# Attention phases of a two-layer kernel: the side work of a phase dealt out over other steps, and the group norm applied on another engine

## The reference, cut to what matters

```python
x = x + _L0_conv_ref(_gn(x), Wq, Wk, Wv, Wo, ln_g, ln_b)
# _gn: group norm, 32 groups of 8 channels over all positions of one image
q = xf @ Wq.T;  k = xf @ Wk.T * SCALING;  vr = xf @ Wv.T        # per head
qr = theta_shift(q, sin_q, cos_q);  kr = theta_shift(k, sin_k, cos_k)
qk = einsum('bhqd,bhkd->bhqk', qr, kr) * mask
den = clip(abs(qk).sum(-1, keepdims=True), 1.0, 50000.0)
out = einsum('bhqk,bhkd->bhqd', qk / den, vr)
out = (out - mu) / sqrt(var + LN_EPS) * ln_g + ln_b             # per head
out = gelu(out) @ Wo.T
```

## Time and profile before

| what | value |
|---|---|
| median of 3 runs | 2482.15 us (2479.42 to 2482.56) |
| the profiled execution | 2484.05 us, span 2482.3 us, granted clock 0.995 |
| PE busy | 2360.1 us, 95% |
| DVE busy | 1811.6 us, 73% |
| ACT busy | 1457.4 us, 59% |
| POOL busy | 1053.4 us, 42% |
| chain that ended last | PE 89%, DVE 7%, issue 2%, ACT 1% |

### The profile page before, as it was taken

How to read it: one execution, slowest core, us unless ns; L and a number is a source line. 1 busy time by engine, 2 the same in 40 slices (tenths; PEclk the granted TensorE clock), 3 DMA queues, 4 the chain that set the end, 5 groups by cost and what they waited for, 6 DMA issues and landing times.

```text
span 2482.3 us, 38646 instructions
## 1 busy us (share of the span) xinstructions
PE 2360.1 (95%) x14870; PEld 1617.3 (65%) x14870; DVE 1811.6 (73%) x2772; ACT 1457.4 (59%) x2063; POOL 1053.4 (42%) x758
## 2 busy tenths in 40 slices
...
GB/s 240 86 73 91 97 88 97 89 97 89 97 90 96 89 97 100 98 66 71 97 94 65 68 111 26 26 26 26 26 26 26 26 26 24 17 17 22 26 26 17
DMA packets 89271, 165.74 MB, mean 67 GB/s; under 512 B 21488, under 2 KB 62840, under 8 KB 80768
## 3 DMA queue, kind: packets, MB, share of 16 engines
...
...
## 4 chain that ended last, share of the span: by engine, by line
PE 89%; DVE 7%; issue 2%; ACT 1%; POOL 0%; another core or an unknown queue 0%; DVEq 0%; POOLq 0%; ACTq 0%
PE scores L1747 9%; PE scores L1745 9%; PE scores L1746 9%; PE scores L418 9%; PE pairC L431 8%; PE pairC L450 5%; PE pairD L347 5%; DVE l_prod L560 4%; PE pairD L356 2%; PE pairC L1745 2%; PE pairC L1746 2%; PE pairC L1747 2%; PE pairD L1745 2%; PE pairD L1747 2%; PE pairD L1746 2%
## 5 line engine op out<-in xcount | busy, mean ns | idle before, releaser
L560 DVE TENSOR_TENSOR l_prod<-scores,l_window 128x1024 f32<-128x1024 f32 x512 | 602.9, 1219 | 198.0 <-PE scores L418 194.4
L773 ACT ACTIVATE l_absp<-l_prod 128x1024 f32<-128x1024 f32 x512 | 539.6, 1055 | 296.1 <-DVE l_prod L560 285.2
L2135 POOL TENSOR_TENSOR e_xnorm<-e_res,e_scale 128x1024 f32<-128x1024 f32 x16 | 38.9, 2434 | 775.3 <-DMA e_res<-t2T_scratch 775.3
L1904 ACT ACTIVATE e_r<-scores,e_bn,e_rs 128x512 f32<-128x512 f32 x256 | 197.9, 779 | 273.2 <-PE scores L1747 273.1
L881 POOL TENSOR_TENSOR l_absp<-l_absp,l_absp 128x1024 f32<-128x1024 f32 x126 | 297.5, 2384 | 5.7 <-ACT l_absp L773 5.7
L2011 DVE CAST e_h1hi<-e_r 128x512 fp32r<-128x512 f32 x256 | 147.7, 577 | 206.4 <-ACT e_r L1904 206.2
L1914 ACT ACTIVATE e_r<-scores,e_bn,e_rs 128x512 f32<-128x512 f32 x250 | 194.7, 781 | 136.8 <-PE scores L1747 135.5
L431 PE MATMUL pairC<-l_prod,l_v 128*32 128x512 f32 x2048 | 270.3, 600 | 0.0
L418 PEld LDWEIGHTS scores<-l_qhi,l_khi 32*128 32x128 f32 x1024 | 49.5, 181 | 319.9 <-DVE l_prod L560 221.2
L2038 DVE TENSOR_TENSOR e_r<-e_r,e_wbc 128x512 f32<-128x512 f32 x250 | 170.8, 691 | 84.8 <-ACT e_r L1914 84.7
L418 PE MATMUL scores<-l_qhi,l_khi 32*128 32x512 f32 x1024 | 129.3, 494 | 96.5 <-DVE l_prod L560 95.8
(11 more groups left out here) (256 smaller groups left out, 5284.3 us busy)
## 6 DMA issues: line engine op xcount, KB each, us to landing
l_absp<-l_absp POOLq DMA_DIRECT2D x63, 1024.0 KB, 7.1
...
l_xa<-x_scratch SPq DMA_DIRECT2D x8, 1024.0 KB, 8.3
l_xr<-x_scratch SPq DMA_DIRECT2D x8, 1024.0 KB, 5.6
t2T_scratch<-l_xt SPq DMA_DIRECT2D x8, 1024.0 KB, 14.9
...
```

The costliest lines, as they stand in the source:

```text
L560: nc.vector.tensor_tensor(prod[2 * (S % 2) + j][:], sc[j][:], win[:, 4 * g + 2 * j:4 * g + 2 * j + 2, w0:w0 + QC], ALU.mult).then_inc(prod ...
L773: nc.scalar.activation(absp[S % ABS][j][:], prod[2 * (S % 2) + j][:], ACT.Abs).then_inc(abs_ready, 1)
L1904: nc.scalar.activation(r1[:, m, :], p1[m], ACT.Relu, bias=bn_[0][1][:, m, n:n + 1], scale=rs[0][:, m, n:n + 1]).then_inc(r1_ready, 1)
```

## The change

- **DMA and POOL pairs.** DMAs now add steps 0+1 and 2+3, POOL 4+5 and 6+7. PE takes the pairs in steps 6, 6, 7 and 9 (in places p=1, where `has_gn` holds, in 5, 7, 7 and 9). The last phase keeps its old split. `weighted` now comes ahead of `sums` in a step.
- **PE side tasks.** v is projected in step 5 (6 where `has_gn` holds). Of the output projections, places 0, 1, 2 and 3 had one, one, two and none; now each has one, in step 4, but for the last two phases.
- **DVE.** head_sums moves from step 2 to step 1, behind the shuffle; centre from 3 to 2; variance from 4 to 3; the residual stands at step 5 ahead of `group_mean`, not at step 6; the image's four `statistics` stand in other steps; `normalise` is gone. `group_mean` has one more small instruction, the negated mean.
- **ACT.** take_num is ahead of absolute(S, 0) in step 0, take_den ahead of it in step 2, squares in step 2, high of k in step 1 of the next phase. `normalise` is here, one activation for each half of the channels, with a shift that POOL makes (`l_gshift`).
- **POOL.** low of k moves behind the last pair of the phase; scale_heads stands between the DMA of 2+3 and the adds of 4+5; the rotation of k behind the adds.
- **Buffers.** t1 and t2 are doubled, one set for q and one for k; the squares have their own buffer; z has a spare piece.

The diff, without the memory map and renamed buffers:

```diff
     def by_dma(P):
-        return (0, 4) if P < PHASES - 1 else (0,)
+        return (0, 2) if P < PHASES - 1 else (0,)
 
     def by_pool(P):
-        return (2, 6) if P < PHASES - 1 else (2,)
+        return (4, 6) if P < PHASES - 1 else (2,)
+
+    def has_gn(P):
+        return P % 4 == 1 and P // 4 + 1 < B
 
     def den_at(P):
 
-        if P < PHASES - 1:
-            return {5: (0, 1), 6: (2, 3), 8: (4, 5), 9: (6, 7)}
-        return {4: (0, 1), 5: (2, 3), 6: (4,), 7: (5,), 8: (6,), 9: (7,)}
-
-    units = sorted((KT * P + at, tuple(KT * P + s for s in steps)) for P in range(PHASES) for at, steps in den_at(P).items())
-    units_at = {at: steps for at, steps in units}
+        if P == PHASES - 1:
+            return ((5, (0, 1)), (5, (2, 3)), (6, (4,)), (7, (5,)), (8, (6,)), (9, (7,)))
+        if has_gn(P):
+            return ((5, (0, 1)), (7, (2, 3)), (7, (4, 5)), (9, (6, 7)))
+        return ((6, (0, 1)), (6, (2, 3)), (7, (4, 5)), (9, (6, 7)))
+
+    units = sorted((KT * P + at, tuple(KT * P + s for s in steps)) for P in range(PHASES) for at, steps in den_at(P))
+    units_at = {S: [steps for at, steps in units if at == S] for S in range(KT * PHASES + 2)}
...
-        return {0: [(b, 0, 0)], 1: [(b, 0, 1)], 2: [(b, 1, 0), (b, 1, 1)], 3: []}[P % 4]
+        if P >= PHASES - 2:
+            return [(b, 1, 0), (b, 1, 1)] if P == PHASES - 2 else []
+        return [(b, P % 4 // 2, P % 2)]
...
             if kt == 5 and len(outs(P)) == 2:
                 out_proj(*outs(P)[1], (part,))
-            if kt == 6 and has_kv(P):
+            if kt == (6 if has_gn(P) else 5) and has_kv(P):
...
-            if S in units_at:
-                sums(units_at[S])
             weighted(S)
+            for steps in units_at[S]:
+                sums(steps)
...
+            nc.vector.tensor_scalar(gneg[:], pA[:, 0:2], -1.0, None, ALU.mult).then_inc(gneg_ready, 1)
...
+            if kt == 1 and has_q(P):
+                shuffle(prep_q(P))
+            if kt == 1 and P > 0:
+                head_sums(P - 1)
+            if kt == 2 and P > 0:
+                centre(P - 1)
             if kt == 3 and P > 0:
-                centre(P - 1)
-            if kt == 4 and P > 0:
+                clip_den(P - 1)
                 variance(P - 1)
-            if kt == 6 and outs(P):
-                add_residual(*outs(P)[-1])
-            if kt == 7 and p == 0 and stats_next:
-                statistics(b + 1, (1,))
+            if kt == 4 and has_kv(P):
+                shuffle(prep_k(P))
+            if kt == 5 and outs(P):
+                add_residual(*outs(P)[0])
+            if kt == 6 and len(outs(P)) == 2:
+                add_residual(*outs(P)[1])
+            if kt == 5 and has_gn(P):
+                group_mean(b + 1, a_order["gn1", P])
+            if kt == 6 and has_gn(P):
+                group_var(b + 1, a_order["gn2", P])
+            if kt in (5, 6, 7) and p == 0 and stats_next:
+                statistics(b + 1, (kt - 5,))
             if kt == 0 and p == 1 and stats_next:
                 statistics(b + 1, (3,))
-            if kt == 1 and has_q(P):
-                shuffle(prep_q(P))
-            if kt == 1 and p == 1 and stats_next:
+            if kt == 2 and p == 1 and stats_next:
                 aggregate(b + 1)
-            if kt == 1 and p == 2 and stats_next:
-                normalise(b + 1, (0,))
-            if kt == 2 and p == 2 and stats_next:
-                normalise(b + 1, (1,))
-            if kt == 2 and P > 0:
-                head_sums(P - 1)
-            if kt == 3 and P > 0:
-                clip_den(P - 1)
-            if kt == 4 and has_kv(P):
-                shuffle(prep_k(P))
-            if kt == 5 and p == 0 and stats_next:
-                statistics(b + 1, (0,))
-            if kt == 5 and has_gn(P):
-                group_mean(b + 1, a_order["gn1", P])
-            if kt == 5 and len(outs(P)) == 2:
-                add_residual(*outs(P)[0])
-            if kt == 6 and has_gn(P):
-                group_var(b + 1, a_order["gn2", P])
-            if kt == 7 and p == 0 and stats_next:
-                statistics(b + 1, (2,))
...
-            if n > 0:
-                act.wait_ge(lo_ready, n)
+            if n > 1:
+                act.wait_ge(lo_ready, n - 1)
             act.wait_ge(a_ready, a + 1)
-            nc.scalar.activation(t1[:], pA[:], ACT.Copy, scale=scale).then_inc(t1_ready, 1)
+            nc.scalar.activation(t1[n % 2][:], pA[:], ACT.Copy, scale=scale).then_inc(t1_ready, 1)
...
-            act.wait_ge(a_ready, a_order["dT", P] + 1)
             act.wait_ge(centred, P + 1)
-            nc.scalar.activation(tB[:], tA[:], ACT.Square, scale=HD ** -0.5).then_inc(sq_ready, 1)
+            nc.scalar.activation(sq[:], tA[:], ACT.Square, scale=HD ** -0.5).then_inc(sq_ready, 1)
+
+        def normalise(b, k):
+
+            act.wait_ge(grstd_ready, 2 * (b + 1))
+            nc.scalar.activation(xn[:, k, :], raw[:, k, :], ACT.Identity, bias=gshift[:, k:k + 1],
+                                 scale=grstd[:, k:k + 1]).then_inc(xn_ready, 1)
 
...
+            b, p = P // 4, P % 4
+            if kt == 0 and P > 0:
+                take_num(P - 1)
+            if kt == 2 and P > 0:
+                take_den(P - 1)
             absolute(S, 0)
             if kt == 1 and has_q(P):
                 take(prep_q(P), a_order["q", P], 1.0)
-            if kt == 2 and P > 0:
-                take_den(P - 1)
+            if kt == 2 and p == 2 and b + 1 < B:
+                normalise(b + 1, 1)
             if kt == 4 and has_kv(P):
                 take(prep_k(P), a_order["k", P], SCALING)
-            if kt == 7 and has_kv(P):
+            if kt == (7 if has_gn(P) else 6) and has_kv(P):
                 v_take(a_order["v", P], (P // 2 + 1) % 2, P % 2)
             absolute(S, 1)
-            if kt == 0 and P > 0:
-                take_num(P - 1)
             if kt == 0 and P > 1:
                 gelu(P - 2)
+            if kt == 1 and P > 0 and has_kv(P - 1):
+                high(prep_k(P - 1))
+            if kt == 1 and p == 2 and b + 1 < B:
+                normalise(b + 1, 0)
+            if kt == 2 and P > 0:
+                squares(P - 1)
             if kt == 2 and has_q(P):
                 high(prep_q(P))
-            if kt == 3 and P > 0:
-                squares(P - 1)
-            if kt == 6 and has_kv(P):
-                high(prep_k(P))
...
+            if P > 0 and has_kv(P - 1):
+                low(prep_k(P - 1))
             pair(P, 0)
             if has_q(P):
                 rotate(prep_q(P), (P + 1) % 2)
                 rotated(prep_q(P))
                 low(prep_q(P))
             pair(P, 2)
+            if P > 0:
+                scale_heads(P - 1)
+            pair(P, 4)
+            if has_gn(P):
+                group_rstd(P // 4 + 1)
             if has_kv(P):
                 rotate(prep_k(P), P % 2)
                 rotated(prep_k(P))
-            pair(P, 4)
-            if P > 0:
-                scale_heads(P - 1)
-            if has_gn(P):
-                group_rstd(P // 4 + 1)
-            if has_kv(P):
-                low(prep_k(P))
```

More of the change, by code:

```diff
@@ L127, in has_kv @@
         return P // 2 + 1 < 2 * B
-    def has_gn(P):
-        return P % 4 == 1 and P // 4 + 1 < B
     def outs(P):
```

50 lines of the change are left out of this document (26 added, 24 removed).

## The result

The changed kernel takes 2511.03 us (median of 4 runs, 2506.92 to 2514.61), the kernel before 2481.48 beside it (4 runs). The ratio is 1.0118, with its interval 1.0105 to 1.0130: slower by 1.2%, 29.5 us. The forecast was 2510.

The account below looks back on a forecast made before the run. PE bounds the kernel: each step lasts its own pass or its wait for products. Terms +45.5 (p=1), -15.9 (p=2), -3.4 (p=0), +2 (last phases) make +28: 2512 profiled, 2510 median; range 2474 to 2528.

Parts of the forecast that it names:

- The tally of steps: PE's eight step lengths in a phase without group norm, summed to 30.36 us, against 30.75 by the same count before.
- step 1: Every phase: head_sums ahead of products(2) waits for PE's transposes, so the step takes 4.62 us, 1.18 more than before.
- The chain: Place p=1: three small group-norm DVE instructions wait in turn for POOL instructions, until about 20.5, 22.9 and 25.3 us.
- step 5: Place p=1: PE waits for DVE's group-norm instructions, idle from 20.6 to 25.4; the step takes 8.1 us.
- The clock's term: Place p=1: PE's idle of 4.8 us lowers TensorE's granted clock, costing 1.6 us, bounds 0 and 3.3.
- seven p=1: The seven group-norm phases: 37.5 us each against 31.02, +6.5 each, +45.5 together.
- Waits priced at nothing: DMA of steps 2+3, adds of 4+5, low of k and normalise on ACT: all taken as covered, cost 0.
- the last phases: The last two phases: head_sums' 1.18 twice, a two-pair step where one was hidden, less one pair: +2 us.
- Rival 1: Group-norm phases: one POOL add is waited out, not two; p=1 at 35.0, total 2493 us; chance 0.22.
- Rival 2: Group-norm phases: DVE meets POOL as before, step 5 is 4.7, no clock falls; total 2475 us; chance 0.16.
- Rival 3: All phases: head_sums costs nothing in step 1, 37 us off the 2475 case; total 2438 us; chance 0.04.
- Rival 4: Ordinary phases: idle in steps 1 and 2 lowers the clock, 1.6 in some 24 phases, +38; 2548 us; chance 0.06.

Follow-up runs that it names:

- c_heads: Kernel after with head_sums back in step 2, centre in 3, variance in 4, squares in 3: 2503.92 us, ratio 1.0080 to the kernel before.
- i_v6: Kernel after, with POOL waiting for l_gvar before the adds of 4+5 (p=1) and v projected in step 6 in every phase: 2501.65 us, ratio 1.0082.
- b_busy: Kernel after plus four PE matmuls of constants while PE would wait for l_gvar, in the seven group-norm phases: 2492.14 us, ratio 1.0029.
- g_one: Kernel after, but POOL waits for l_gvar between the two halves of the adds of 4+5, in group-norm phases: 2489.97 us, ratio 1.0023.
- a_wait: Kernel after, but POOL waits for l_gvar before starting the adds of 4+5, in the seven group-norm phases: 2466.68 us, ratio 0.9928.
- h_norm: a_wait with the group norm applied by DVE again in steps 1 and 2 of place p=2, not by ACT: 2489.44 us, ratio 1.0023.

## Why the prediction was right, point by point

**The tally of steps held.** Forecast for the ordinary phase: 3.79, 4.62, 3.44, 3.79, 3.79, 3.86, 3.63, 3.44, in all 30.36. Measured in p=0 between the starts of scores from 287.99 on: 3.82, 4.61, 3.52, 3.82, 3.82, 3.88, 3.61, 3.44, in all 30.52. The two rows that set step 1, DVE and PE of the kernel after, stand as the forecast put them:

```profile
293.41 0.69 DVE L580 TENSOR_REDUCE l_nsum<-pairD 128x16 f32<-128x512 f32 x1 [0.67 <-PE pairD L380]
...
296.42 0.51 PE L429 MATMUL scores<-l_qhi,l_khi 32*128 32x512 f32 x4 [1.19 <-DVE l_prod L572]
```

Step 2 came out 0.08 longer than 3.44, as it already was before (3.52). c_heads shows that head_sums is the cause of step 1, i_v6 that full steps add up.

**The chain waits out POOL one for one.** Forecast: to 20.5, 22.9 and 25.3 after the phase's start, step 5 at 8.1. From 318.51 on the three instructions ended at 20.4, 22.7 and 25.0, and without the clock's part step 5 is 7.57 (b_busy); with one add waited out it is 5.43 (g_one, second image) for the 5.7 forecast. The Trainium skill ("SBUF — State Buffer", section "Who interferes with whom") gives the exclusion; a_wait and g_one agree with it, each add taken out of the way giving back one instruction's 2.1 us. The rows of layer 1 were weaker ground than I took them for: the second DVE row is a cast with one operand, and only the first is of the kind that waits here.

**The clock's term was mis-sized.** Forecast 1.6 in p=1, with ends 0 and 3.3. b_busy against the kernel after gives 2.7 to 3.0 from the second image on, in the phase shown some 1.9 in step 5 (9.47 less 7.57) and 0.9 in step 6 (4.74 less 3.88). The 1.6 was read behind an idle of 2.63, and g_one has the same 1.6 behind 2.3. Behind 4.4 the low level lasted longer, and I had said that it "should do the same". By scores, p=1 is 38.1 (318.51 to 356.64) for the 37.4 that the forecast's terms add up to (it says 37.5): the clock +1.2, the wait -0.5. The two errors have opposite signs, which is luck.

**The account by starts of scores.** Marks mislead here, as said above, so the forecast is held against the starts of scores, which are the same point of the program in both kernels.

| part | before | after | difference | forecast |
|---|---|---|---|---|
| up to the start of phase 1 | 62.27 | 61.29 | -1.0 | -0.7 |
| seven p=1 | 217.0 | 266.0 | +49.0 | +45.5 |
| seven p=2 | 229.6 | 213.3 | -16.3 | -15.9 |
| seven p=3 | 212.7 | 212.5 | -0.2 | 0 |
| seven p=0 | 216.1 | 213.6 | -2.5 | -2.7 |
| phases 29 and 30 | 65.1 | 63.2 | -1.8 | +2 with the next row |
| phase 31 up to its last scores | 20.6 | 22.5 | +1.9 | |
| all behind that | 1458.8 | 1460.4 | +1.6 | 0 |

Together +30.6 for +28. The terms fit nearly as well as the end value. The seven p=1 cost 3.5 more, the last phases cost nothing where +2 was put, and 1.6 came behind the last scores of layer 0, for which the forecast has no term.

**Waits priced at nothing.** None shows: in the ordinary phases PE has no other wait for an engine than those of steps 1 and 2, 1.19 and 0.97, and the profile shows no wait of PE for a DMA. But the word on low of k was too short. It is in time for the scores, as I wrote; that POOL's list waits for it (2.38 in the kernel after) and rotates q behind it costs nothing only as long as step 1 is long, and 0.8 a phase after that (c_heads).

**The rivals.** Rival 1 fell with g_one, which is that case built on purpose: p=1 at 34.9 by starts of scores and the total 2490, for the 35.0 and 2493 that I gave it. Rival 2 is what a_wait makes; at ratio 0.9928 it is a better kernel than the 2475 I gave it, because with the chain free step 5 is 3.43 and not 4.7: the old hold-up of l_gvar goes as well. Rival 3 needed a second edit. Rival 4 did not occur: in the kernel after all seven p=0 take 30.49 to 30.52, and a_wait, with all the ordinary waits of 1.19 and 0.97, has a granted clock of 0.996.

What stays open: why one idle of 2.26 left the clock alone (g_one) and others of 2.33 and 2.28 did not (g_one, h_norm), and why the idle of 2.63 in phase 0 was followed by the low level in nine kernels and not in h_norm. The length of the idle alone does not decide it. No run was made for it.
